# The output bias and the softmax branch of a fused two-layer transformer move from GpSimd into TensorE's output projection

## What is computed

```python
xn = _layernorm(x)
x1 = x + attn0(xn) + ffn0(xn)          # first layer
#   attn0: 16 heads; cosine scores, 1 - arccos(.)/pi to the 16th power, normalised;
#          then  out @ Wo.T + bo                       <- output projection and its bias
#   ffn0:  16-head softmax attention (attn_out) + 8 experts, the best 2 mixed (moe_out)
xn1 = _layernorm(x1)
y = x1 + attn1(xn1) + ffn1(xn1)        # causal attention; FP4-rounded gate/up/down
```

## Time and profile before

| what | value |
|---|---|
| median of 3 runs | 1997.37 us (1996.66 to 2009.59) |
| profiled execution, from its first to its last instruction (span) | 2001.0 us |
| busy DVE, ACT, PE, POOL | 1799.0, 1773.5, 1475.5, 1189.6 us |
| steps in the loop | 28 in 14 rounds, some 57 to 63 us each |

### The profile page before, as it was taken

One profiled execution on the slowest core, in us unless ns is written; L12 is line 12 of the kernel. 1 busy time (PEld: TensorE's weight loads), 2 busy tenths in 40 slices (PEclk: granted clock), 3 DMA queues, 4 the chain that ended last, 5 costly groups with the idle time before them and its releaser, 6 DMA issues.

```text
span 2001.0 us, 38650 instructions
## 1 busy us (share of the span) xinstructions
PE 1475.5 (74%) x12022; PEld 748.7 (37%) x12022; DVE 1799.0 (90%) x4073; ACT 1773.5 (89%) x1888; POOL 1189.6 (59%) x547
## 2 busy tenths in 40 slices
PE   2677777777777777787777777687777768777765
PEld 1223333433343433344334333343333434333433
DVE  5779999999999999999999999999999999999874
ACT  2299998999989999899989999899998999989894
POOL 1566665666656666566665666566666566656640
PEclk9677988888888998889988888888988899988876
DMA  1000000000000000000000000000000000000000
GB/s 41 4 3 1 6 1 5 6 6 6 6 5 0 6 6 6 6 6 3 3 6 5 6 6 6 0 6 6 5 6 6 6 0 6 6 5 6 4 4 6
DMA packets 21058, 11.19 MB, mean 6 GB/s; under 512 B 1431, under 2 KB 20953, under 8 KB 20956
## 3 DMA queue, kind: packets, MB, share of 16 engines
q1 hardware_dynamic: 20956, 10.20, 1.8%
HBM read 6.00 MB, written 4.19 MB: 5 GB/s over the span
## 4 chain that ended last, share of the span: by engine, by line
ACT 40%; DVE 21%; issue 21%; PE 15%; DVEq 1%; ACTq 1%; SPq 0%; DMA 0%; POOL 0%
ACT curve L559 23%; ACT root L559 7%; PE psM L1024 3%; PE psM L1177 3%; DVE nmax L872 3%; ACT prob L559 2%; ACT L590 2%; PE psV L1208 2%; DVE h L433 1%; DVE stkT L858 1%; ACT p L559 1%; PE psS L1082 1%; DVE xqT L427 1%; DVE curve L862 1%; DVE oh L826 1%
## 5 line engine op out<-in xcount | busy, mean ns | idle before, releaser
L511 POOL TENSOR_TENSOR root<-curve 128x2048 f32<-128x2048 f32 x128 | 478.9, 3742 | 452.4 <-DVE curve L866 452.4
L559 ACT ACTIVATE curve<-curve 128x2048 f32<-128x2048 f32 x384 | 716.1, 1906 | 4.5 <-POOL curve L514 2.3
L559 ACT ACTIVATE root<-root 128x2048 f32<-128x2048 f32 x256 | 484.5, 1906 | 0.0
L514 POOL TENSOR_TENSOR curve<-curve,root 128x2048 f32<-128x2048 f32 x64 | 353.7, 5539 | 109.5 <-ACT root L559 109.5
L866 DVE TENSOR_SCALAR curve<-psS 128x1024 f32<-128x1024 f32 x256 | 308.0, 1214 | 1.9 <-PE psS L1055 1.9
L872 DVE TENSOR_REDUCE nmax<-psS 128x4 f32<-128x1024 f32 x256 | 302.9, 1214 | 2.4 <-PE psS L1064 2.4
L559 ACT ACTIVATE prob<-psS 128x1024 f32<-128x1024 f32 x256 | 257.0, 1031 | 24.2 <-PE psS L1084 22.2
L547 POOL TENSOR_TENSOR stk<-qk,stk 128x512 f16<-128x512 f32 x128 | 151.2, 1192 | 67.7 <-ACT stk L559 67.3
L1064 PE MATMUL psS<-stkT 32*128 32x256 f16 x1024 | 107.2, 307 | 87.5 <-DVE stkT L858 39.5
L1208 PE MATMUL psV<-curve,vc 128*32 128x256 f32 x2048 | 142.2, 410 | 35.1 <-ACT curve L559 31.4
L862 DVE TENSOR_TENSOR curve<-curve,root 128x2048 f32<-128x2048 f32 x64 | 156.9, 2452 | 6.1 <-ACT root L559 6.1
(11 more groups left out here) (197 smaller groups left out, 2861.4 us busy)
## 6 DMA issues: line engine op xcount, KB each, us to landing
xt<-in_L_attn_x SPq DMA_DIRECT2D x32, 128.0 KB, 2.2
out<-yo SPq DMA_DIRECT2D x32, 128.0 KB, 1.8
we<-in_L_ffn_W_experts SPq DMA_DIRECT2D x1, 512.0 KB
curve<-in_L_attn_w_qkv SPq DMA_DIRECT2D x1, 192.0 KB
curve<-in_L_ffn_w_down SPq DMA_DIRECT2D x1, 176.0 KB
curve<-in_L_ffn_w_gate SPq DMA_DIRECT2D x2, 64.0 KB
curve<-in_L_ffn_w_up SPq DMA_DIRECT2D x2, 64.0 KB
curve<-in_L_ffn_W_qkv SPq DMA_DIRECT2D x1, 128.0 KB
```

What stands on the lines that cost most here:

```text
L511: nc.gpsimd.tensor_tensor(root[:, two], curve[:, p, two], curve[:, p, two], ALU.mult).then_inc(s_sq, 1)
L514: nc.gpsimd.tensor_tensor(curve[:, p, two], curve[:, p, two], root[:, two], ALU.mult).then_inc(s_half[0], 1)
L559: return nc.scalar.activation(out, in_, func, **kw)
```

## The change

The five parts of `x1` are kept; who adds them changes.

- Stage `wo` on PE: each token tile gets three matmuls into the same part of the bank instead of one: a row of ones by the bias row (1 partition), the identity by `of` (128x128, f32), and the projection as before. It now also waits for `finf` of the same sequence.
- DVE's first expert (e = 0) reads `xt` where it read `acc`. `experts` waits for the sequence's landing and for `x1` of two sequences before, two waits in place of the one for `residual`.
- GpSimd's `residual` and `fadd` go, and with them their semaphores; `finf` on DVE waits for the projection of the sequence before (`s_wop`), `wo` on DVE for the experts (`s_moe`).
- At the start of the program the bias is no longer spread over the partitions: one matmul and one copy less; `bo` is loaded into a row of its own, and the row of ones has a place of its own.
- The one list `SCHEDULE` becomes one list per engine (`ORDER`); but for the two stages that go, each engine's list holds its stages in the order in which they stood before.

```diff
-SCHEDULE = [
-    ("table", 0, -1), ("c", 2, 0), ("s1", 0, -2), ("wln", 0, -1), ("fadd", 0, -1), ("finf", 0, -1), ("wln", 1, -1),
...
+ORDER = {
+    "sync": [
+        ("load", 0, 1), ("down", 0, -2),
...
-        BIAS_ROWS = [(brow[0:1, 0:3 * D + E], wfb[:, :]), (brow[0:1, 3 * D + E:], bob[:, :])]
+        BIAS_ROWS = [(brow[0:1, :], wfb[:, :])]
...
-                if stage == "residual":
-
-                    pool.wait_ge(s_x[p], due(s_x[p], b, LANDED[p]))
-                    pool.wait_ge(s_x1, due(s_x1, b - 2))
-                    nc.gpsimd.tensor_tensor(acc[:, p, :, :], xt[:, p, :, :], bc(bob[:, :], 1, NT), ALU.add).then_inc(s_acc0, 1)
...
-                if stage == "fadd":
-                    pool.wait_ge(s_finf, due(s_finf, b))
-                    pool.wait_ge(s_moe, due(s_moe, b))
-                    nc.gpsimd.tensor_tensor(acc[:, p, :, :], acc[:, p, :, :], of[:, :, :], ALU.add).then_inc(s_acc2, 1)
...
                 if stage == "experts":
-                    dve.wait_ge(s_acc0, due(s_acc0, b))
+                    dve.wait_ge(s_x[p], due(s_x[p], b, LANDED[p]))
+                    dve.wait_ge(s_x1, due(s_x1, b - 2))
                     dve.wait_ge(s_gate, due(s_gate, b))
...
+                        so_far = xt if e == 0 else acc
                         nc.vector.scalar_tensor_tensor(acc[:, p, j, :], bank[:, (e % 4) * D:(e % 4 + 1) * D],
-                                                       comb[:, p, j, e:e + 1], acc[:, p, j, :], ALU.mult,
+                                                       comb[:, p, j, e:e + 1], so_far[:, p, j, :], ALU.mult,
                                                        ALU.add).then_inc(s_moe, 1)
...
                 if stage == "finf":
-                    dve.wait_ge(s_acc2, due(s_acc2, b - 1))
+                    dve.wait_ge(s_wop, due(s_wop, b - 1))
...
                     dve.wait_ge(s_wop, due(s_wop, b))
-                    dve.wait_ge(s_acc2, due(s_acc2, b))
+                    dve.wait_ge(s_moe, due(s_moe, b))
...
                     pe.wait_ge(last, value)
+                    pe.wait_ge(s_finf, due(s_finf, b))
                     pe.wait_ge(s_ocT, due(s_ocT, b))
                     for j in range(NT):
-                        ins = mm(bank[:, j * D:(j + 1) * D], ocT[:, j * P:(j + 1) * P], woT[:, :], start=True, stop=True)
+                        out = bank[:, j * D:(j + 1) * D]
+                        mm(out, onerow[:, :], borow[:, :], start=True, stop=False)
+                        mm(out, ident[:, :], of[:, j, :], start=False, stop=False)
+                        ins = mm(out, ocT[:, j * P:(j + 1) * P], woT[:, :], start=False, stop=True)
                     ins.then_inc(s_wop, 1)
```

More of the change, by code:

```diff
@@ L80 @@
+MOST_LAG = max(-lag for order in ORDER.values() for s, a, lag in order)
+LAG = {(s, a): lag for s, a, lag in ORDER["tensor"]}
 USES = {"xnT": 1, "proj": 2, "maxT": 1, "finc": 1, "ocT": 1, "wo": 1, "xn1T": 1, "p1": 2, "s1": 1, "p1T": 1, "o1": 1,
         "xqT": 1, "gu": 2, "finf": 1, "stackT": 1, "experts": 2, "hT": 1, "down": 1}
-MISC = [(s, a, use) for s, a, lag in SCHEDULE for use in range(USES.get(s, 0))]
-SCORES = [(s, a, 0) for s, a, lag in SCHEDULE if s in ("c", "m", "e")]
+MISC = [(s, a, use) for s, a, lag in ORDER["tensor"] for use in range(USES.get(s, 0))]
@@ L86 @@
+SCORES = [(s, a, 0) for s, a, lag in ORDER["tensor"] if s in ("c", "m", "e")]
 assert len(SCORES) % 2 == 0
@@ L141, in build @@
         wfb = sb("wfb", [P, 3 * D + E])
-        bob = sb("bob", [P, D])
+        borow = sb("borow", [1, D])
+        onerow = sb("onerow", [1, P])
         we = sb("we", [P, E, D])
@@ L233, in build @@
         wfl = spare[:, 52 * D:54 * D]
-        brow = spare[0:1, 32 * D:32 * D + 4 * D + E]
+        brow = spare[0:1, 32 * D:32 * D + 3 * D + E]
         bload = spare[0:3, 40 * D:40 * D + E * D]
@@ L387, in build, with steps @@
         block = ctx.enter_context(nc.Block())
-        def steps(eng, run):
+        def steps(eng, order, run):
             def step(t, parity):
-                for stage, arg, lag in SCHEDULE:
+                for stage, arg, lag in order:
                     if not isinstance(t, int) or 0 <= t + lag < B:
@@ L399, in steps @@
                     step(i * 2 + (2 + k), k)
-            for t in range(B - 2, B - min(LAG.values())):
+            for t in range(B - 2, B + MOST_LAG):
                 step(t, t % 2)
@@ L454, in _ @@
             sp.dma_start(brow[:, 3 * D:3 * D + E], b_gate.rearrange("(a n) -> a n", a=1)).then_inc(s_w, 16)
-            sp.dma_start(brow[:, 3 * D + E:], bo.rearrange("(a n) -> a n", a=1)).then_inc(s_w, 16)
+            sp.dma_start(borow[:, :], bo.rearrange("(a n) -> a n", a=1)).then_inc(s_w, 16)
             def run(stage, arg, b, p, t):
@@ L464, in run @@
                     sp.dma_start(y_flat[bass.ds(at, T * D)].rearrange("(j p d) -> p j d", p=P, d=D), yo[:, p, :, :]).then_inc(s_out[p], 16)
-            steps(sp, run)
+            steps(sp, ORDER["sync"], run)
             for b in (B - 2, B - 1):
@@ L489, in _ @@
                 link(nc.gpsimd.memset(iota8[:, e:e + 1], float(e)))
-            link(nc.gpsimd.memset(ones1, 1.0))
+            link(nc.gpsimd.memset(onerow[:, :], 1.0))
             link(nc.gpsimd.memset(unity[:, :], 1.0))
@@ L547, in run @@
                     nc.gpsimd.tensor_tensor(lo, src, hi, ALU.subtract).then_inc(s_stk, 1)
-                if stage == "fadd":
-                    pool.wait_ge(s_finf, due(s_finf, b))
-                    pool.wait_ge(s_moe, due(s_moe, b))
-                    nc.gpsimd.tensor_tensor(acc[:, p, :, :], acc[:, p, :, :], of[:, :, :], ALU.add).then_inc(s_acc2, 1)
-            steps(pool, run)
+            steps(pool, ORDER["gpsimd"], run)
         @block.scalar
@@ L712, in run @@
                     activate(hqT[:, j, :, :].rearrange("p c q -> p (c q)"), bank[:, 0:NCH * P], ACT.Copy).then_inc(s_hT, 1)
-            steps(act, run)
+            steps(act, ORDER["scalar"], run)
         @block.vector
@@ L980, in run @@
                                             x2[:, :, :], ALU.add).then_inc(s_y, 1)
-            steps(dve, run)
+            steps(dve, ORDER["vector"], run)
         @block.tensor
@@ L1001, in _ @@
                 else:
-                    mm(bank, ones1, src, start=True, stop=True).then_inc(s_wps, 1)
+                    mm(bank, onerow[:, :], src, start=True, stop=True).then_inc(s_wps, 1)
             pe.wait_ge(s_wcp, SETUP_USES)
@@ L1211, in pv @@
                 ins.then_inc(done, 1)
-            steps(pe, run)
+            steps(pe, ORDER["tensor"], run)
 INPUTS = ["L0_attn_x", "L0_attn_Wq", "L0_attn_Wk", "L0_attn_Wv", "L0_attn_Wo", "L0_attn_bo", "L0_ffn_W_qkv",
```

65 lines of the change are left out of this document (40 added, 25 removed), and 3 rows, old and new, of the table ORDER.

## The result

The changed kernel takes 2055.3 us, the median of 4 runs (2032.43 to 2081.33), against 1998.15 for the kernel before beside it. Two of its four runs, 2074.56 and 2081.33, had a lower granted clock throughout and are left out of the comparison: the ratio of the others to the kernel before is 1.0165, with a 95% interval of 1.0121 to 1.0209. The change made the kernel slower by 1.7%, where 1.5% faster was forecast. The profiled execution has a span of 2034.2 us, 33.2 more than before.

A forecast was written before the change was run, and what follows sets the result against it. DVE and ACT, busy nine tenths of the span and handing work to each other, were taken as the bound. Terms +19 + 0 - 49 = -30 us against the 2001.0 span gave 1967 us, -1.5%, range 1954 to 2022.

The forecast's parts named there:

- first term: TensorE's projection between `ocT` and `x1`: 0.89 us more, less 0.25 ACT has in hand; 0.6 per step, +19 us.
- upper price of 1.95 us: Projection's eight added instructions at the slowest similar rate found, 0.24 us each: upper end of that cost, +62 us.
- The term for the stalls: First halves of the loop body: added waits shift DVE's code, so they take 56.96 us like second halves; -49 us.
- The gap at line 419: DVE in first halves: 0.24 us "issue" idle, 14 times, read as a code-block change that makes DVE late and starts stalls.
- the boundary: DVE's code-block crossing, predicted to fall two to four instructions earlier, before or inside the Newton step (lines 805 to 807).
- GpSimd's additions at 0: Removing GpSimd's two 0.73 us additions per step saves nothing, since GpSimd idles 2.24 us behind the first for ACT's sigmoid.
- The bound below, -46.7: GpSimd's removed additions: lower end of their effect, in us over the run, if some engine waited for all of it.
- the stalls stay: First rival: gap remains at line 419, only the added cost is left, 2016 us; chance 0.19.
- the second: Rival: `mul` 0 and DVE's line 826 collide more often, seven more stalls, 2047 us; chance 0.13.
- The third's case: Rival: line 419 free, but line 826 still meets GpSimd's product in three or four of 28 steps; 1987 us; chance 0.10.
- line 441, line 839, `xqT` and GpSimd's 47 us: Signs: line 419 no idle, near 0.17 us; line 826 near 160 ns; `xqT` without 5 us waits; GpSimd busy 47 less.
- The projection's 1.6 us, DVE's 0.8 and ACT's 0.6: Signs: PE's projection some 1.6 us in 12 instructions; DVE idle about 0.8 before `x1`, ACT about 0.6 before `lnv`.

The follow-up runs named there:

- a1_wait: Kernel before with one more, long-past wait for the sequence's landing in each experts stage on DVE; 1973.45 us, ratio 0.9848.
- b2_ahead: Kernel before with DVE's first two waits issued four times, three more instructions ahead of the loop, loop body unchanged; 1977.36 us, ratio 0.9899.
- a5_fold_fadd: Changed kernel with the old four-instruction projection: bias put into the softmax branch's value bias, GpSimd adds that branch, first expert reads `x`; 1978.36 us, ratio 0.9832.
- a2_nowait: Changed kernel without the experts stage's second wait, for the landing, so DVE's loop body is as long as before; 2032.93 us, ratio 1.0155.
- b3_zeros: Kernel before with one more wait per experts stage and the change's added projection matmuls fed zeros, both GpSimd additions kept; 2057.34 us, ratio 1.0301.
- a3_k128: Changed kernel with the bias added as identity times a 128-partition bias tile, same 12 instructions per projection, all 128 rows; 1999.69 us, ratio 0.9968.
- a8_onewait: Changed kernel with the experts stage's landing wait kept only once in the loop, in its first half, first four experts; 2037.75 us, ratio 1.0144.

## Why the prediction was wrong

**Its first term was mis-sized: "eight instructions at 0.11 us", +0.6 us per step, +19 us.** The 0.11 came from two projection instructions of the earlier trace rows that follow others of the same 128 rows. It holds for the kernel whose added matmuls all have 128 rows (1.58 us for 12). In the change, 1 row and 128 rows alternate, and the projection takes 2.15 us at the full clock: 1.47 more than before, where 0.89 was reckoned. The rest of that term was right for steps at the full clock: taking off ACT's 0.25 us in hand gives the shortest step of the first five kernels of the table. Those steps all have a granted clock of 0.91 over the step. The run with the bias alone has no such step with its projection at the full clock; its shortest, at 0.85, is 0.83 us longer than the sum.

| kernel | projection at full clock | 56.85 + projection - 0.68 - 0.25 | shortest step seen | mean of 26 steps of the loop |
|---|---|---|---|---|
| before, one wait more | 0.68 | 56.85 (start of the sum) | 56.85 | 58.05 |
| softmax branch alone on TensorE | 1.13 | 57.05 | 57.09 | 57.99 |
| bias with 128 rows | 1.58 | 57.50 | 57.55 | 58.81 |
| other order | 1.97 | 57.89 | 57.92 | 58.17 |
| the change | 2.15 | 58.07 | 58.07 | 59.82 |
| bias alone on TensorE | 1.70 | 57.62 | 58.45 | 59.29 |

So at the full clock the change costs 58.07 - 56.85 = 1.22 us a step, some 39 us, twice the term.

**What the sum had no term for is the clock.** The change's shortest step is 58.07, but the mean over the loop is 59.82 us, 1.75 more; in the other order it is 58.17, only 0.25 more, and with one wait more in the kernel before 58.05, 1.20 more than its shortest. In the second of the windows above the lower clock falls on the projection, where nothing hides it: everything on DVE and ACT waits there for TensorE. That is a part only. DVE's wait for the projection is 68.9 us in the change and 49.1 in the other order, 20 us of the 48 between their spans:

```profile
DVE x L928 <- PE psM L1139: 49.1, 32, 3.9
```

ACT's wait for the softmax scores goes from 41.6 to 17.5 us between the same two. The prediction knew that the clock changes and used it only for which steps stall; its upper price of 1.95 us for the added instructions, +62 us, was taken for an end of the range that would hardly come about.

**The term for the stalls had its mechanism right and its size wrong: "the first halves then take what a second half takes, -49 us".** The gap at line 419 was what started the stalls of the kernel before, and a shift of the code removes both: 28 us less with a1_wait, 25 with b2_ahead. The kernel without stalls does not have steps of 56.96 us throughout, though; its mean is 58.05, as the lower clock then falls into other waits, on the scores and the second `proj`. Where the boundary would go, in front of the Newton step or into it, was not borne out: no gap is seen there.

**GpSimd's additions at 0** held where the projection is short (a5_fold_fadd), and not where it is long: there the rest of the change, their going in it, is worth 20 us of span, 10 of them seen at line 436. The bound below, -46.7, held that. The waits and the first expert's `x` are 0, as said, as far as a2_nowait and a5_fold_fadd can tell.

In the spans, the profiled executions add up: -28 for the stalls (a1_wait), +81 for the projection (b3_zeros), -20 for the rest of the change: +33. Against the forecast's +19, 0 and -49, the miss of 63 us is 62 for the longer projection, with what it does to the clock, 21 for the stalls and 20 the other way for the rest, GpSimd's part.

The rivals: none had the right cause. That the stalls stay or come more often did not happen, although the second gave the number nearest to the result, 2047; that is luck. The third's case, a free line and stalls all the same, was seen with a3_k128 and not in the change. Of what was to be seen, line 441, line 839, `xqT` and GpSimd's 47 us were right. The projection's 1.6 us, DVE's 0.8 and ACT's 0.6 in front of it and of `lnv`, and the steps of 57 to 58 were wrong, and GpSimd's idle time before `mul` fell, from 109.5 to 86.4 us, where more was expected.

Shown by runs: the gap's part in the stalls of the kernel before; the alternation's price; that the projection alone brings the loss. What stays open: what decides on which stretch the lower clock falls. Length alone does not: the run with 1.58 us per projection (1999.69) is slower than the one with 1.97 (1987.16), though two of its steps also stall. Not tried: issuing the four added matmuls ahead of the wait for `ocT`, which they do not read.

The fastest version of the study is the kernel before with one redundant wait in each experts stage, 1973.45 us: 1.5% faster than the kernel before, and the change takes 1.0165 / 0.9848 = 1.032 times as long as it.

## What to carry to other kernels

A price per matmul from a row of equal matmuls does not carry over to a mixture: look for rows where shapes alternate, and if none exists, put the alternation itself into the range. Work added to TensorE between two engines that both wait for it should be priced at both levels of the clock, and the order of matmuls within one bank is worth a run of its own: here it was 48 us. When a few instructions of padding move a kernel by more than 1%, as here, look for a race between two engines, and measure the gain or loss of an edit nearby against a padded kernel before.

## What the runs showed of the hardware that was not expected

- Each change between f32 matmuls of 1 row and of 128 rows costs 0.19 us at the full clock, in the mean: 12 instructions in 1.58 us with no change, 1.97 with two, 2.15 with three. At a change the weight load begins with its matmul, behind a matmul of the same shape 0.11 us ahead of it (873.70 and 873.71, 873.28 and 873.39 in the change).
- DVE's instruction stream has places with a gap of 0.19 to 0.28 us, which go with the place in the code: one instruction less in front of the line moved the gap behind it, three more ahead of the loop moved it elsewhere and the kernel by 24 us. One shift of five, a8_onewait, did not fit a fixed count. The Trainium skill (Runtime: NRT & Kernel Launch, "Instruction fetch mechanics") calls the crossing of a block mostly hidden; in the kernel before it was not, at one place met 14 times, and that decided 28 us; that is, if a block is what these gaps are, which no run here shows.
- A single 0.73 us addition on GpSimd held up a 0.41 us operation of DVE that began 0.26 us later: it took 0.75 us and was done 0.28 us behind the addition (726 ns in the mean of all steps).
